# The router's 32 token groups in chunks of 4, 8, 8, 8 and 4, before 8, 8, 8 and 8

## What is computed

```python
probs = softmax(xf @ gate_w.T)             # [4096, 8]
order = argsort(-probs)                    # per token
csum = cumsum(p_sorted)
select_prefix = arange(E) <= argmax(csum >= 0.9)
R = where(select_prefix, p_sorted - rank, -1e9)   # scattered back to expert order
keep = the 512 tokens with the largest R, per expert
scores = where(assign_mask & keep, probs, 0)
y = sum over e of scores[:, e] * (gelu(xf @ w1[e].T) @ w2[e].T)
out = x + y
```

## Time and profile before

| | us |
|---|---|
| median of three runs | 282.74 (281.26 to 282.98) |
| the profiled execution's own time | 284.87 |
| its span | 283.1 |
| TensorE busy | 244.9 (87%) |
| VectorE busy | 208.1 (74%) |
| ScalarE busy | 151.8 (54%) |

### The profile page before, as it was taken

How to read it: one execution, slowest core, us unless ns; L and a number is a source line. 1 busy time by engine, 2 the same in 40 slices (tenths; PEclk the granted TensorE clock), 3 DMA queues, 4 the chain that set the end, 5 groups by cost and what they waited for, 6 DMA issues and landing times.

```text
span 283.1 us, 3852 instructions
## 1 busy us (share of the span) xinstructions
PE 244.9 (87%) x1326; PEld 183.9 (65%) x1326; DVE 208.1 (74%) x505; ACT 151.8 (54%) x281; POOL 144.5 (51%) x104
## 2 busy tenths in 40 slices
PE   0868858665489999999999999999999999999980
PEld 0645423212248888788888888888888888888760
DVE  5299977998955897799789779869977966951330
ACT  6331205686134774676587377468657746754200
POOL 0000000000877258858867885885888587583521
PEclk9995868675759999999999999999999999999997
DMA  6999989910348026925973792594498259054520
GB/s 233 426 424 416 495 306 389 335 47 2 111 128 356 3 74 211 263 48 147 320 128 86 289 220 47 170 300 83 111 312 171 77 208 162 8 77 67 148 111 37
DMA packets 12482, 53.38 MB, mean 189 GB/s; under 512 B 2720, under 2 KB 2976, under 8 KB 9248
## 3 DMA queue, kind: packets, MB, share of 16 engines
q1 hardware_dynamic: 4208, 35.31, 34.1%
q0 software_dynamic: 8256, 17.85, 28.0%
HBM read 44.63 MB, written 17.96 MB: 221 GB/s over the span
## 4 chain that ended last, share of the span: by engine, by line
PE 73%; DVE 13%; DMA 4%; ACT 3%; issue 3%; POOL 2%; POOLq 0%; SPq 0%; ACTq 0%; DVEq 0%
PE bank L762 21%; PE bank L763 20%; PE bank L764 20%; PE bank L742 4%; PE bank L824 2%; ACT region L405 2%; DVE xg L589 2%; DMA xg<-in_x,gath 2%; DMA region<-in_xt 2%; DVE region L637 2%; POOL xg L255 1%; PE bank L803 1%; PE bank L758 1%; DVE csum L595 1%; DVE rank L593 1%
## 5 line engine op out<-in xcount | busy, mean ns | idle before, releaser
L255 POOL DMA_INDIRECT xg<-in_x,gath x32 | 51.7, 1617 | 97.4 <-DVE gath L525 69.9
L469 DVE SCALAR_TENSOR_TENSOR w1rot<-w1raw,rot,w1rot 128x512 f32<-128x512 f32 x84 | 63.1, 751 | 5.1 <-ACT w1rot L308 3.1
L270 POOL DMA_INDIRECT out<-ysb,scat x32 | 53.8, 1680 | 19.8 <-DVE ysb L711 8.0
L762 PE MATMUL bank<-w2h,hh 128*128 128x512 f32 x128 | 51.7, 404 | 0.0
L762 PE MATMUL bank<-xh,w1h 128*128 128x512 f32 x128 | 50.9, 398 | 0.0
L763 PE MATMUL bank<-xl,w1h 128*128 128x512 f32 x128 | 50.1, 391 | 0.0
L764 PE MATMUL bank<-w2h,hl 128*128 128x512 f32 x128 | 50.0, 391 | 0.0
L764 PE MATMUL bank<-xh,w1l 128*128 128x512 f32 x128 | 50.0, 390 | 0.0
L763 PE MATMUL bank<-w2l,hh 128*128 128x512 f32 x128 | 49.9, 390 | 0.0
L498 DVE TENSOR_TENSOR hl<-hf,hh 128x512 fp32r<-128x512 f32 x32 | 22.0, 689 | 32.5 <-ACT hh L339 32.5
L335 ACT ACTIVATE hf<-bank 128x512 f32<-128x512 f32 x32 | 19.1, 598 | 40.2 <-PE bank L764 40.2
(11 more groups left out here) (128 smaller groups left out, 331.5 us busy)
## 6 DMA issues: line engine op xcount, KB each, us to landing
region<-in_xt SPq DMA_DIRECT2D x8, 1024.0 KB, 9.1
w1raw<-in_w SPq DMA_DIRECT2D x8, 1024.0 KB, 9.1
w2raw<-in_w SPq DMA_DIRECT2D x8, 1024.0 KB, 4.8
xg<-in_x,gath POOLq DMA_INDIRECT x32, 3.7
score<-probs_scratch,pidx POOLq DMA_INDIRECT x32, 2.8
out<-ysb,scat POOLq DMA_INDIRECT x32, 7.2
ch<-in_ch SPq DMA_DIRECT2D x1, 368.5 KB, 7.8
cf<-in_cf SPq DMA_DIRECT2D x1, 149.0 KB, 2.2
```

The lines of the kernel that those rows point to most:

```text
L255: pool.indirect_dma_start(xg[:, s, :], None, x_d, bass.IndirectOffsetOnAxis(gath[:, e, s:s + 1], 0)).then_inc(xg_in[s], 16)
L270: pool.indirect_dma_start(out_d, bass.IndirectOffsetOnAxis(scat[:, e, s:s + 1], 0), ysb[:, s, :], None, compute_op=ALU.add if e < LAST els ...
L469: ins = nc.vector.scalar_tensor_tensor(dst, w1raw[:, e % 2, i, :], rot[:, j, i:i + 1], dst, ALU.mult, ALU.add)
L762: nc.tensor.matmul(dst, ah, bh, start=first, stop=False)
```

## The change

Chunks get the sizes 4, 8, 8, 8 and 4, so there is a fifth. It needs a fifth place for its logits, `bank[0]`, which chunk 0 used; TensorE therefore waits for chunk 0's centring before it writes there. `count_ranks` is called for five chunks, and the wait for all centrings moves ahead of `fold(1, 0)`, which writes `bank[0]`. ScalarE's loop over CHUNKS puts `exp(0)` behind the first parts copy, `exp(1)` behind the third, `exp(2)` behind the fifth, `exp(3)` behind the seventh and `exp(4)` behind the eighth (before: behind the second, fourth, sixth and eighth). Chunk c now starts when gate group 0, 2, 4, 6 or 7 is transposed (before: 1, 3, 5, 7).

```diff
--- before.py
+++ after.py
@@ -41,7 +41,7 @@
 TG = 512
 NG = N // TG
 TPG = TG // P
-CHUNKS = ((0, 8), (8, 16), (16, 24), (24, 32))
+CHUNKS = ((0, 4), (4, 12), (12, 20), (20, 28), (28, 32))
 GW = 32
 XRING = 4
 KV, KA = 4, 3
@@ -168,7 +168,7 @@
         xbank, hbank, ybank = bank[0:2], bank[2:4], bank[4:6]
         vbank = bank[6][:, 0:S4 * NR].rearrange("p (s r) -> p s r", r=NR)
         x0bank = lambda s: bank[(0, 1, 4, 5)[s]][:, :].rearrange("p (c n) -> p c n", c=C4)
-        pbank, lbank, rbank = bank[1:3], [bank[i] for i in (0, 3, 5, 7)], bank[4]
+        pbank, lbank, rbank = bank[1:3], [bank[i] for i in (0, 3, 5, 7, 0)], bank[4]
         fbank, kbank, cbank, obank, dbank = [bank[i] for i in (6, 0, 3, 5)], bank[7], bank[1:3], bank[3], bank[7]
 
         starts_of = lambda n, e0, e1: (obank[:, 0:2 * (e1 - e0)] if n == 0 else
@@ -808,6 +808,8 @@
                 pe.wait_ge(parts_ev, g + 1)
                 c = next(c for c, (lo, hi) in enumerate(CHUNKS) if lo <= g * TPG < hi)
                 at = g * TPG * GW - CHUNKS[c][0] * GW
+                if c == 4:
+                    pe.wait_ge(centred, 1)
                 nc.tensor.transpose(lbank[c][:, at:at + P], parts[:, g % 2, :], ident).then_inc(logits_mm, 1)
 
             def count_ranks(c):
@@ -839,11 +841,11 @@
             pe.wait_ge(w1_in[0], 16)
             for i in range(C4):
                 fold(0, i)
-            count_ranks(2)
-            count_ranks(3)
+            for c in range(2, len(CHUNKS)):
+                count_ranks(c)
+            pe.wait_ge(centred, len(CHUNKS))
             fold(1, 0)
             fold(1, 1)
-            pe.wait_ge(centred, len(CHUNKS))
 
             pe.wait_ge(cf_in, 16)
             pe.wait_ge(key_ready, 1)
```

## The result

The changed kernel takes 284.5 us (median of seven runs, 283.99 to 285.25), the kernel before, run beside it, 282.98 (seven, 281.26 to 283.64). The ratio is 1.0066, 95% interval 1.0038 to 1.0094: 1.1 to 2.7 us slower. Weighted by their executions (7 and 12) the two differences of means, +1.87 and +1.17, give +1.43 us, with a standard error of about 0.25; the forecast was +1.42 and 284.2. Two kernels of the experiments had one or two executions of over 480 us, which are left out of every mean.

The account below looks back on a forecast made before the run. VectorE was taken to bound the routing, whose end moves all that follows. Last levels +1.63 us less 0.21 for fewer rank counts gave +1.42, from 282.74 to 284.2; range 282.2 to 286.0.

Parts of the forecast that it names:

- What bounds the routing: VectorE bounds routing from first chunk to last, 6.49 us per chunk of eight; its end moves all that follows.
- The early start: Chunk 0 needs only one gate group, so VectorE starts it at 10.00 us, 2.74 earlier.
- The floor under chunk 1: Chunk 1 needs the third transpose of logits, ending at 15.70, so it can't start before 15.74 us.
- the predicted wait of 0.68: VectorE, done with chunk 0 at 15.06, would wait 0.68 us for gate group 2.
- signs that the prediction named for being wrong: Third transpose well before or after 15.7, chunk 0 overrunning it, or a different clock between 38 and 46 us.
- What a small chunk costs: On VectorE a chunk of four takes 5.06 us, not 6.49; the last reaches its levels in 4.71, not 6.07.
- What is moved: ScalarE's new order, TensorE's moved waits and the later store of the probabilities (landing at 63) cost nothing.
- The clock at the folds: After a pause of 4.7 us TensorE's two folds meet a clock of 0.50 again, adding nothing against the profiled execution.
- Rival 2: Earlier timed runs met the folds at full clock and the longer pause takes it away: +1.42 + 1.7, 285.9; chance 0.14.
- The 1.42 of the sum: Last chunk's levels 1.63 us later, less 0.21 for four rank-count matmuls instead of eight: net +1.42 us.
- Rivals 1, 3 and 4: Folds at full clock, 282.5 or 281.5 (0.10); small chunks save little, 286.3 (0.04); almost no loss left, 283.2 or 282.5 (0.12).
- rival 4: Clock rises sooner in the folds, first threshold round held less: +0.4, 283.2; or last chunk at 3.04, 282.5; together 0.12.

Follow-up runs that it names:

- the pair with the clock held: Idle matmuls ahead of the last rank count: 14 in the kernel before, 0.9981; 18 in the changed kernel, 1.002; both ratios against the kernel before.
- both pairs: Kernel before and changed kernel, each with idle matmuls in TensorE's pause (0.9981, 1.002), and each with all of fold 1 there (0.9964, 1.0003).
- 4, 4, 8, 8, 8: Changed kernel with these chunk sizes, last chunk of eight: 1.0073 against the kernel before; with fold 1 also in TensorE's pause: 0.9994.

## Why the prediction came out right

**What bounds the routing.** Right. Chunks of eight take 6.48 to 6.50 us in every trace, and where the folds behind met the same clock, what the counts lose is found again at the first expert matmul (0.43 and 0.42 for the change, 1.50 and 1.44 for the pair with the clock held).

**The early start.** Right in itself, 9.84 to 10.18 in the traces. The floor under chunk 1, the third transpose, is right where the gates run at the lower clock (15.70, wait 0.67). Where they run at the higher one the third transpose is done by 14.57 to 14.85, and chunk 1 starts when chunk 0 ends, at 14.84 to 15.15. Both traces of the changed kernel itself are of this kind. So the predicted wait of 0.68 isn't in them, and one of the signs that the prediction named for being wrong, a third transpose well before 15.7, came up. The prediction took the gates' speed for given; the clock column, which says 1.00 there, gave no warning. What the change costs at the counts therefore depends on the execution: 1.3 us in one pair and 0.8 in the other, both with the start of the first gate taken out, and 1.0 in the means of both pairs.

**What a small chunk costs.** Right: 4.97 (5.06), 4.63 to the levels (4.71), four counts for eight 0.21 cheaper (38.99 to 39.20).

**What is moved.** Right: +0.15 us for TensorE's waits and the bank, the store landing at 62.5. ScalarE's new order wasn't run alone; in the traces of the change it holds up no chunk.

**The clock at the folds.** The forecast that it is 0.50 held in the profile. The two traces of the changed kernel differ: 3.76 and 3.47 us for the two folds behind the last count, and 46.57 and 45.64 for the first round's count. That the level met is partly chance follows from what the Trainium skill says of a monitor that runs freely ("TensorE: Matmul & The Clock Gate", "What's actually happening"); these traces agree. Rival 2, a share of the loss from folds that meet the full clock less often behind a longer pause, can't be ruled out. 4, 4, 8, 8, 8 lost 1.65 us with the folds on the path and 0.79 with them off it, each against the chunks of before with its folds in the same place; the change itself lost 1.43 and 1.02. Both surpluses, 0.86 and 0.4, point the same way, but with some 0.5 of uncertainty on each it isn't shown. The executions point there too: of the 99 of before that ran beside the experiments, 14 had a mean granted clock of 0.926 and took 281.4 in the mean, which 1.4 us more would put at 282.8; none of the 19 of the changed kernel has that clock, and none took less than 283.16. The 1.42 of the sum was thus met by an arithmetic of about 1.0 and, likely, a few tenths of this. That it met 1.43 to a hundredth is luck, with a standard error of 0.25 on the measured value.

**Rivals 1, 3 and 4.** No execution of the changed kernel was faster than 283.16. The small chunks did save what was said. The round ahead of which TensorE was late gave back little in the profile: its count ran at 46.57 for 46.22. In the second trace it did what rival 4 says, 45.64 with the counts 0.77 later, and still the mean stayed 1.2 to 1.9 us above before.

## What to carry to other kernels

An earlier first step is worth only what is left of it after the next wait for data, and here the small first chunk brought a fifth chunk, whose fixed costs are all on the path: price the extra set of fixed costs first. Where one engine is the bound and its data arrives in steps, choose the pieces so that the last piece starts when the last data arrives; three chunks of 8, 12 and 12 gained 1.3 us where five of 4, 8, 8, 8 and 4 lost 1.4. Look at what another engine does just behind the last step: the folds there were worth nearly as much as the best chunk sizes.

## What was not expected of the hardware

The granted clock reads 1.00 from the start of each trace until it first falls, although the first matmuls run at the lower level: in the trace after, 32 of them take 1.91 us at the start, 1.08 later with 1.00, 1.93 with 0.50. The durations have to be looked at, not the column alone. And the time of one unchanged kernel on one core spreads by 4 us (280.86 to 284.92 in 35 executions), and much of that goes with the clock's pattern: of the 99 executions, the 14 with a mean granted clock of 0.926 took 281.1 to 282.3 us, the five with 0.916 took 284.5 to 284.9. (The mean alone doesn't order them: the four with 0.933 took 283.2 to 283.6.) So one profile can lie 1.7 us from the median, and two profiles compared with each other told 0.3 us where the means said 1.4.
